# A graph kernel on one core: variance on one row, moved ranges of cells, all equal-key counts in the edge stage

## What is computed

```python
# layer 0: edge convolution, attention mix, norm, mixture of 8 experts
e = relu((x[dst] - x[src]) @ theta.T + phi(x[src]));  out = segment_max(e, dst)   # "runs" of edges
h = layernorm(x_joined);  w = softmax(h @ Wr + br);   y = sum_e w_e * expert_e(h)
# layer 1: three SAGE layers on the same graph
mean = segment_sum(h[src], dst) / max(deg, 1);  h = relu(mean @ Wl + h @ Wr)
```

## Time and profile before

| | before |
|---|---|
| median of 3 runs (lowest, highest) | 2259.45 us (2256.13, 2262.32) |
| the profiled execution: its time / its span | 2258.26 / 2256.5 us |
| busy PE / DVE / POOL / ACT, of the span | 77% / 59% / 50% / 27% |
| granted TensorE clock, mean over the span | 0.85 |
| cells: `DMA_INDIRECT` L715 | 400, 1311 ns each |
| gathers: `DMA_INDIRECT` L281 | 400, 1237 ns each |

### The profile page before, as it was taken

One profiled execution on the slowest core, in us unless ns is written; L12 is line 12 of the kernel. 1 busy time (PEld: TensorE's weight loads), 2 busy tenths in 40 slices (PEclk: granted clock), 3 DMA queues, 4 the chain that ended last, 5 costly groups with the idle time before them and its releaser, 6 DMA issues. The chain is left out here.

```text
span 2256.5 us, 25514 instructions
## 1 busy us (share of the span) xinstructions
PE 1740.6 (77%) x8349; PEld 1011.8 (45%) x8349; DVE 1320.1 (59%) x2672; ACT 598.0 (27%) x940; POOL 1122.8 (50%) x888
## 2 busy tenths in 40 slices
PE   7984645544553658999999628699989999996996
PEld 6962222211222434555555427555565555544543
DVE  6877866776674666777777515445541221125996
ACT  4001101110110135666666312211220010003453
POOL 0868888888885737888888768400000000000344
PEclk9557877777775669999999858799999999997998
DMA  6346788878886202111220200344325433431002
GB/s 173 85 134 195 212 225 230 216 216 219 217 215 163 54 10 61 35 34 34 34 34 9 67 1 2 52 103 109 100 50 130 124 95 92 127 80 38 0 4 82
DMA packets 193283, 229.05 MB, mean 102 GB/s; under 512 B 66688, under 2 KB 174292, under 8 KB 187811
## 3 DMA queue, kind: packets, MB, share of 16 engines
q1 hardware_dynamic: 126001, 172.58, 29.0%
q0 software_dynamic: 67200, 55.46, 11.1%
HBM read 148.81 MB, written 78.24 MB: 101 GB/s over the span
## 5 line engine op out<-in xcount | busy, mean ns | idle before, releaser
L715 POOL DMA_INDIRECT adjacency<-all_cell_val,all_cell_idx x400 | 524.5, 1311 | 173.5 <-issue 121.0
L281 POOL DMA_INDIRECT edge_ring<-b_rows,all_src_idx x400 | 494.8, 1237 | 187.0 <-issue 168.1
L1742 POOL TENSOR_TENSOR ffn_hl<-ffn_hid,ffn_hh 128x448 f16<-128x448 f32 x56 | 70.1, 1254 | 717.3 <-ACT ffn_hid L1759 717.1
L1555 PE MATMUL bank<-sage_adj,sage_zh 125*128 125x448 f16 x1050 | 370.1, 352 | 3.4 <-DVE sage_zl L1609 3.4
L1555 PE MATMUL bank<-sage_adj,sage_zl 125*128 125x448 f16 x1050 | 370.0, 352 | 0.0
L535 DVE SCALAR_TENSOR_TENSOR edge_ring<-edge_ring,w_keep 125x256 f32<-125x256 f32 x399 | 193.0, 484 | 128.6 <-DMA edge_ring<-b_rows,all_src_idx 112.8
L1201 ACT ACTIVATE bank<-bank,w_shift,w_scale 128x448 f32<-128x448 f32 x224 | 147.1, 697 | 76.7 <-PE bank L728 76.7
L1632 DVE TENSOR_TENSOR sage_u<-bank,w_rd 128x448 f32<-128x448 f32 x42 | 26.2, 625 | 236.2 <-PE bank L1560 233.4
L1555 PEld LDWEIGHTS bank<-sage_adj,sage_zh 125*128 125x128 f16 x1050 | 102.6, 98 | 101.9 <-issue 8.0
L1555 PEld LDWEIGHTS bank<-sage_adj,sage_zl 125*128 125x128 f16 x1050 | 102.7, 98 | 99.6 <-issue 5.8
L690 DVE SCALAR_TENSOR_TENSOR edge_junk<-bank,all_key_c,all_later 125x400 f16<-125x400 f32 x232 | 145.7, 628 | 0.0
(11 more groups left out here) (433 smaller groups left out, 3448.3 us busy)
## 6 DMA issues: line engine op xcount, KB each, us to landing
sage_adj<-adjacency SPq DMA_DIRECT2D x105, 490.0 KB
run_max<-edge_ring SPq DMA_DIRECT2D x40, 1120.0 KB
adjacency<-edge_zero SPq DMA_DIRECT2D x25, 714.0 KB
experts_gb<-gate_rows SPq DMA_DIRECT2D x56, 224.0 KB, 3.3
edge_ring<-b_rows,all_src_idx POOLq DMA_INDIRECT x400, 7.1
adjacency<-all_cell_val,all_cell_idx POOLq DMA_INDIRECT x400, 2.6
sage_adj<-adjacency SPq DMA_DIRECT2D x105, 56.9 KB
run_max<-edge_ring SPq DMA_DIRECT2D x40, 130.0 KB
```

The lines of the kernel that those rows point to most:

```text
L281: nc.gpsimd.indirect_dma_start(ring[:, k % RING, :], None, dram.rows[:, :], bass.IndirectOffsetOnAxis(ap=c.src_idx[:, k:k + 1], axis=0)).t ...
L715: nc.gpsimd.indirect_dma_start(dram.adj_flat, bass.IndirectOffsetOnAxis(ap=c.cell_idx[:, k:k + 1], axis=0), c.cell_val[:, k:k + 1], None). ...
L1555: ins = mm(ps[4 * b + h][:, 0:T], z[:, g * JG + j, half(h)], adj[g][:, j, :], start=(g == 0 and j == 0 and z is zh), stop=False)
L1742: nc.gpsimd.tensor_tensor(hl[:, m, :], hid[:, m, :], hh[:, m, :], ALU.subtract).then_inc(low, 1)
```

## The change

1. In the edge stage DVE does all 400 counts, 1.18 for each scan from number 60 on in place of 0.68. When count 320 has been issued, `make_cells` is called for columns 0 to 319 (FIRST = 320), and after the last scan for the other 80.
2. The experts stage has no counts, no `make_cells` and no wait of POOL for them.
3. The ranges of cells: 56 columns in the join (46 before), 254 beside the experts (244), 58 beside norm2 (45), 32 beside mix1 (65).
4. The variance of the join: PE multiplies the squares as weights with one column of `mean_w`, so that a group of 4 blocks gives 125x4 numbers in place of 128x500. ACT's root goes to `sd`, DVE's reciprocal to `rs` (125x4), and PE spreads `rs` with 4 transposes into bank 4, for which DVE's scaling waits (`rs_spread`).

```diff
-JOINED = 46
-LATE = 3 * NT * NEXP
+JOINED = 56
...
-    COUNTS = L - LATE
-    counts_by = lambda k: (k - SCANS) * COUNTS // (L - SCANS)
+    FIRST = 320
+    counts_by = lambda k: (k - SCANS) * L // (L - SCANS)
...
                         count_equal(v, dve, c, ps[3][0:B, 0:L], j, j, junk[:, j % 2, :], counted)
+                        if j == FIRST:
+                            dve.wait_ge(counted, FIRST + 2)
+                            make_cells(v, count_step, c, cell[:], dup[:], slice(0, FIRST))
...
-                make_cells(v, count_step, c, cell[:], dup[:], slice(0, COUNTS))
+                dve.wait_ge(counted, L + 2)
+                make_cells(v, count_step, c, cell[:, FIRST - L:], dup[:, FIRST - L:], slice(FIRST, L))
...
-                        if g >= 1:
-                            act.wait_ge(scaled, g)
-                        nc.scalar.activation(ps[4][:, 0:wide(g)], ps[3][:, 0:wide(g)], ACT.Sqrt, bias=c.eps5[:, 0:1]).then_inc(sd_ready, 1)
+                        if g >= 2:
+                            act.wait_ge(rs_ready, g - 1)
+                        nc.scalar.activation(sd[:, g % 2, 0:size(g)], ps[3][0:B, 0:size(g)], ACT.Sqrt, bias=c.eps5[0:B, 0:1]).then_inc(sd_ready, 1)
...
-                        v.reciprocal(ps[4][:, 0:wide(g)], ps[4][:, 0:wide(g)]).then_inc(rs_ready, 1)
+                        if g >= 2:
+                            dve.wait_ge(rs_spread, g - 1)
+                        v.reciprocal(rs[:, g % 2, 0:size(g)], sd[:, g % 2, 0:size(g)]).then_inc(rs_ready, 1)
...
-                        dve.wait_ge(rs_ready, g + 1)
+                        dve.wait_ge(rs_spread, g + 1)
...
+                    if t >= 3:
+                        g = t - 3
+                        pe.wait_ge(rs_ready, g + 1)
+                        if g >= 1:
+                            pe.wait_ge(scaled, g)
+                        for j in range(size(g)):
+                            ins = nc.tensor.transpose(ps[4][:, B * j:B * (j + 1)], rs[:, g % 2, j:j + 1].to_broadcast([B, P]), c.ident[0:B, 0:B])
+                        ins.then_inc(rs_spread, 1)
...
-                        product(nc, ps[3][:, 0:wide(g)], [c.mean_w[:]] * KH, [sq[:, k, 0:wide(g)] for k in range(KH)]).then_inc(var_done, 1)
+                        for j in range(size(g)):
+                            ins = product(nc, ps[3][0:B, j:j + 1], [sq[:, k, B * j:B * (j + 1)] for k in range(KH)], [c.mean_w[:, 0:1]] * KH)
+                        ins.then_inc(var_done, 1)
...
-                        if steps == K:
-                            for i in range(3 * e, 3 * e + 3):
-                                count_equal(v, dve, c, c.key_c[:], 3 * K * t + i + L - LATE, 3 * K * t + i, junk[:, i % 2, :], counted)
-                    if steps == K:
-                        step.turn(t, 7)
-                        dve.wait_ge(counted, 3 * K * t + 3 * K + 2)
-                        make_cells(v, step, c, cell[:], dup[:], bass.ds(L - LATE + 3 * K * t, 3 * K))
-                        dve.sem_inc(made, 1)
...
-            experts(nc, c, w, dram, made, lambda pool: place_cells(nc, c, dram, pool, JOINED, 290, made))
+            experts(nc, c, w, dram, lambda pool: place_cells(nc, c, dram, pool, JOINED, 310))
...
-                norm(nc, c, 2, lambda pool: place_cells(nc, c, dram, pool, 290, 335), [
+                norm(nc, c, 2, lambda pool: place_cells(nc, c, dram, pool, 310, 368), [
...
-            mix1(nc, c, w, qT, ctx, lambda pool: place_cells(nc, c, dram, pool, 335, L))
+            mix1(nc, c, w, qT, ctx, lambda pool: place_cells(nc, c, dram, pool, 368, L))
```

More of the change, by code:

```diff
@@ L184, in edges @@
             sb = lambda name, shape, dt=F32: late.enter_context(nc.sbuf_tensor(f"cells_{name}", shape, dt))
-            cell, dup = sb("cell", [B, COUNTS]), sb("dup", [B, COUNTS])
+            cell, dup = sb("cell", [B, FIRST]), sb("dup", [B, FIRST])
         free = c.a.rearrange("p k n -> p (k n)")
@@ L672, in _ @@
                     v.tensor_tensor_scan(full[:, h, :], w.reset[:], ps[h][:, 0:B], -BIG, ALU.min, ALU.max).then_inc(ends_scanned, 1)
-                dve.wait_ge(counted, COUNTS + 2)
-                make_cells(v, count_step, c, cell[:], dup[:], slice(0, COUNTS))
+                dve.wait_ge(counted, L + 2)
+                make_cells(v, count_step, c, cell[:, FIRST - L:], dup[:, FIRST - L:], slice(FIRST, L))
 def take(nc, act, c, ps, turned, taken, g, n):
@@ L703, in make_cells, with place_cells @@
     step(v.tensor_tensor(c.cell_val[:, at], c.cnt[:, at], dup, ALU.mult))
-def place_cells(nc, c, dram, pool, first, last, made=None):
-    per = LATE // NT
+def place_cells(nc, c, dram, pool, first, last):
     for k in range(first, last):
-        if made and k >= L - LATE and (k - L + LATE) % per == 0:
-            pool.wait_ge(made, (k - L + LATE) // per + 1)
         if k >= WP * PB and k % WP == 0:
@@ L890, in join_norm_gate @@
         br = s.sb("br", [B, NEXP])
+        sd, rs = s.sb("sd", [B, 2, 4]), s.sb("rs", [B, 2, 4])
         br_in, hot_ready, spread = s.sem("br_in"), s.sem("carry_hot"), s.sem("carry_spread")
@@ L894, in join_norm_gate @@
         mean_done, centred, sq_ready, var_done = s.sem("mean_done"), s.sem("centred"), s.sem("sq_ready"), s.sem("var_done")
-        sd_ready, rs_ready, scaled = s.sem("sd_ready"), s.sem("rs_ready"), s.sem("scaled")
+        sd_ready, rs_ready, rs_spread, scaled = s.sem("sd_ready"), s.sem("rs_ready"), s.sem("rs_spread"), s.sem("scaled")
         high, lowed, logits = s.sem("y_high"), s.sem("y_low"), s.sem("logits")
@@ L1107, in _, with experts @@
                     ins.then_inc(w_turned, 1)
-def experts(nc, c, w, dram, made, beside):
+def experts(nc, c, w, dram, beside):
     with Scope(nc, "experts") as s:
@@ L1115, in experts @@
         gT = s.sb("gT", [NEXP, T])
-        junk = s.sb("junk", [B, 2, L], F16)
-        cell, dup = s.sb("cell", [B, LATE // NT]), s.sb("dup", [B, LATE // NT])
-        counted, own_c = s.sem("counted"), s.sem("cell_steps")
         h1h, h1l = s.sb("h1h", [P, 2, KH, T], F16), s.sb("h1l", [P, 2, KH, T], F16)
@@ L1262, in tile @@
                             ins.then_inc(dm, 1)
-                        if steps == K:
-                            for i in range(3 * e, 3 * e + 3):
-                                count_equal(v, dve, c, c.key_c[:], 3 * K * t + i + L - LATE, 3 * K * t + i, junk[:, i % 2, :], counted)
-                    if steps == K:
-                        step.turn(t, 7)
-                        dve.wait_ge(counted, 3 * K * t + 3 * K + 2)
-                        make_cells(v, step, c, cell[:], dup[:], bass.ds(L - LATE + 3 * K * t, 3 * K))
-                        dve.sem_inc(made, 1)
-                dve.sem_inc(counted, 2)
-                step = Steps(dve, own_c)
                 tile(0)
@@ L1922, in build @@
                                                 pieces(f[0], w.Wo, mats[2])), plan)
-            made = g.sem("cells_made")
-            experts(nc, c, w, dram, made, lambda pool: place_cells(nc, c, dram, pool, JOINED, 290, made))
+            experts(nc, c, w, dram, lambda pool: place_cells(nc, c, dram, pool, JOINED, 310))
         with Scope(nc, "w2") as g:
```

## The result

| | before | changed |
|---|---|---|
| median of 20 runs (lowest, highest) | 2260.73 us (2256.13, 2264.1) | 2266.74 us (2262.07, 2270.86) |
| ratio, 95% interval | 1 | 1.0026 (1.0019 to 1.0032) |
| the profiled execution: its time / its span | 2258.26 / 2256.5 us | 2269.08 / 2267.3 us |
| busy PE / DVE / POOL / ACT, of the span | 77% / 59% / 50% / 27% | 77% / 57% / 50% / 26% |

What follows compares the result with a forecast made beforehand. Bounds differed by stage: POOL in edges, norm2 and mix1, a ring of engines in the join, nearly a tie in experts. Terms 1.4 - 15.5 + 24.4 - 11.1 = -0.8 us gave 2258.7 us, range 2250 to 2270.

Steps and rivals of the forecast that it cites:

- The counts among the gathers: Edge stage: added counts mostly fit in DVE's waits for gathers; +1.4 us, bounds 0 and +20.
- The join: Join: narrow reciprocal and root, transposes beneath DVE's join, less a clock loss; -15.5 us, bounds -8 and -20.5.
- In one or two of five: Join: share of iterations where PE's clock rises late, each losing 2.1 us; taken as +3 us.
- Experts: Experts: POOL's 254 columns plus holds end the stage; +6.9 us, less 1.9 of waiting.
- 30 us of holds: Experts: POOL calls held by 56 subtractions, by laying calls 1.49 us apart; POOL ends 410 us after its start.
- the 1.9 us that it waited beyond a barrier of 2.9 are gone: End of experts: POOL, now last, no longer waits beyond the barrier; -1.9 us.
- norm2: norm2, bounded by POOL alone: 13 more columns at 1.49 us; +19.4 us.
- mix1: mix1: with 32 columns POOL is out of the way, and DVE and a 2.9 us barrier end it; -11.1 us.
- The columns keep their 1.65 us: Rival, experts: POOL ends 420 us after its start, not 410; +9.9 us, 2268.6; chance 0.10.
- Counts hold the gathers: Rival, edge stage: counts hold POOL's gathers as they hold columns; 10 us added, 2268.7; chance 0.05.
- The clock falls behind: Rival, join: PE's clock is late in every iteration; saving 8, not 15.5 us, 2266.2; chance 0.12.
- stays up: Rival, join: PE's clock stays up as idle time shrinks; saving 20.5 us, 2253.7; chance 0.10.

Runs made afterwards that it cites:

- Experiments 5: Changed kernel with the 1.6 MB load of the carry rows issued ten scans earlier; ratio 0.9987 to the kernel before.
- 6: Changed kernel with the same 400 counts done by scan 370, none among the last 30 scans; ratio 0.9986 to the kernel before.
- 10: Changed kernel with one SBUF input, not two, in the operation making the join's low parts; ratio 0.9994 to the kernel before.
- experiment 7: Changed kernel with the experts' subtraction (two SBUF inputs) replaced by a multiplication by 0.0 with one; ratio 0.9958 to the kernel before.
- 8: Changed kernel with columns split 56 join, 246 experts, 36 norm2, 62 mix1; 2228.6 us, ratio 0.9862 to the kernel before.
- experiment 1: Changed kernel with the ranges and wide variance of before, so only the counts moved; ratio 1.0007 to the kernel before.
- experiments 2: Kernel before with only the narrow variance added; ratio 0.9907 to the kernel before.
- 4: Changed kernel with the old ranges (46, 244, 45, 65 columns); ratio 0.9928 to the kernel before.

## Why the prediction was wrong, point by point

**The counts among the gathers: +1.4 forecast, +7.5 in the trace.** This is one of the two steps that failed. The prices and DVE's wait were right (34 us left, 39 forecast). Wrong was "DVE's largest lag grows by about 1.5 us, and its last scan is 0.9 us later". I laid the new scans against the landings of the old trace, as if these were fixed. They are not: the load that starves the gathers is issued behind scan 370, and with DVE later it was issued at 654.38 in place of 648.20. The long wait then ended 8.9 us later (672.52 against 663.61), 20 scans before the end, and each of these scans costs DVE 1.1 us of the 1.5 that POOL gives it: 0.4 us won back by each, 8 in all, for a lag that had just grown by the wait. All eight traces with 400 counts and this tail have a wait of 3.8 to 8.0 us with 21 to 23 scans left and none of over 1 us in the last 20; all three with 232 counts have two or three there. Experiments 5 and 6 show it from two sides, the load moved or the tail bare: waits come back near the end, so DVE had caught up. The size varies by execution: the last scan came 5.0, 5.2 and 5.4 us after the last call in the three kernels with 232 counts, and 5.8 to 9.6 (mean 7.6) in the eight with 400 and an unchanged tail; the stage took 696.2 (694.3 to 698.7) against 700.5 us (696.3 to 703.2) in the mean. So the counts cost about 4 us in this stage, and 7.5 in the trace shown; how much of the difference between the two is chance stays open.

**The join: -15.5 forecast, -14.4.** The size was right, its make-up was not. The other engines gained 21.0 us (130.0 against 151.0 up to the last low part), above my bound of 20.5, and POOL gave 6.6 back with a mechanism that I had seen beside the experts and not looked for here: its ten more columns reach into four operations with two SBUF inputs. The long call is 5.7 of the 6.6. I had POOL end 15 us after 813.5, so at 828.5, or 836 with the later start of the join; it ended at 839.97. The long call (5.55 to 6.89 us) is in all four traces in which POOL was still placing then, and in none of the six others with 56 or 50 columns, where POOL was done. That these operations cause it is argued from that and from where the calls end: 1.06 to 1.07 us after the end of the third operation in three traces (0.26 before the end of the fourth), after the end of the fourth in the one of 6.89, by the same rule as beside the experts. Why the call does not get in between the first and the second stays open; the kernel that was to show the cause (10) missed the place. "In one or two of five" for the slow clock held in the two traces of the changed kernel; of the first five variances one and two ran wholly at half clock there, up to four in the other narrow joins. The variance of the changed kernel at 784.80 us, and the next reciprocals:

```profile
784.80 3.36 PE L764 MATMUL bank<-all_mean_w,join_sq 128*125 128x1 f32 x16
...
788.49 0.18 DVE L1007 RECIPROCAL join_rs<-join_sd 125x4 f32<-125x4 f32 x1 [7.31 <-ACT join_sd L947]
```
```profile
801.91 0.18 DVE L1007 RECIPROCAL join_rs<-join_sd 125x4 f32<-125x4 f32 x1 [5.94 <-ACT join_sd L947]
```

3.36 us is half clock (granted 0.50); at full clock the wide variance took 1.84. The two iterations that took 16.7 us each take 13.4 to 15.1, with the clock down in all or most of them. But the two before them, 18.1 and 17.6 us in the wide form, take 10.8 to 17.1, by whether the clock is up (17.1 where the variance that ends them is at half clock): there is the gain that I had not forecast, and most of the spread of 136 to 145 us among the narrow joins.

**Experts: +5.0 forecast, +12.7.** The second step that failed, by two sizes. "30 us of holds" was 36.8 here, and 29.8 to 32.8 in four other executions with the same 254 columns without counts. POOL took 416.0 us here, 408.8 to 412.0 in those, where I had said 410: the middle was met and I left it no spread. That was partly luck. Laid again by what the traces show (a call that begins within the operation ends 1.06 us after it), calls 1.49 us apart give 22 us of holds against the 56 starts of the trace with counts, which I had used, and 38 against those of the changed kernel; why the other executions have 30 to 33 the laying does not tell. Nor does the phase run freely: 32 of the 49 calls that begin in the subtraction do so 0.04 to 0.13 us after its start, since the fourth call after such a one again falls just behind the next start, 6.81 us later.

And "the 1.9 us that it waited beyond a barrier of 2.9 are gone" was wrong: POOL is idle 4.63 us though it is last, hardly less than its 4.84 before. So this step was wrong in every execution: the experts took 413.4 to 420.6 us in the five traces, 415.9 in the mean, +8.0 for the +5.0 forecast. DVE starts 3.92 us after POOL's last call (1264.80 less 1260.88), but 1.13 to 1.30 after its own last work where it is last (mix1 here, the experts of experiments 7 and 8). So the end of a call of POOL is not yet its arrival at the barrier, and POOL had in effect been last before too: DVE had been idle 2.20 us there, not 1.3. First before, then experiment 7:

```profile
1259.03 0.08 DVE L839 MEMSET all_a<- 128x22 f16 x1 [2.20 <-PEq L83]
```
```profile
1248.42 0.08 DVE L838 MEMSET all_a<- 128x22 f16 x1 [1.30 <-PEq L82]
```

The counts' own holds, 10 us by my laying, were small: in the trace of before 3.2 of the 39.0 us fall on the calls (16) that met a count and not the subtraction. But without counts the other calls fall elsewhere too, and POOL's time fell by 5.7 us in experiment 1 and, for 244 columns, from 403.7 to 391.9 between experiments 2 and 4. That the subtraction holds the calls is shown by where they end, and by experiment 7: 36.8 us became 7.1. The Trainium skill, SBUF — State Buffer, section "Who interferes with whom", says that a VectorE instruction with at most one SBUF input outside the modes with two ports leaves GpSimd alone. The trace agrees for inputs from PSUM: none of 137 calls was held by a count with its keys there. The multiplication of experiment 7, with one SBUF input, held all 27 that began in it; whether it ran in such a mode no run here shows.

**norm2: +19.4 forecast, +19.5.** 13 columns at 1.49 us in a stage that POOL alone holds. Right.

**mix1: -11.1 forecast, -13.4.** Right in mechanism; I took 2.9 us for the barrier after DVE, and DVE is idle only 1.13 us.

**The rivals.** "The columns keep their 1.65 us" nearly came true in the first trace, 1.64 (416.0/254), and less in the others, 1.61 to 1.62. "Counts hold the gathers": POOL's calls are busy 3.1 us more in the edge stage, 1.7 in the mean of the eight traces, not 10, and by scans, not by counts. "The clock falls behind" came true for two iterations, "stays up" for two others. In sum: 6.1 and 7.7 us too little (edges, experts), 1.1 too much gain for the join, 0.1 too little for norm2, and 2.3 and 1.0 us of the other sign (mix1, the rest), which turns the -0.8 of the forecast into +10.9, and the spans differ by 10.9. Of these 10.9 us some 5 to 9 are this pair of executions and not the change, since the medians of the two sets differ by 6.0 and 1.2 to 1.8.

## What to carry to other kernels

Where one stream of work is laid against the waits of another, look at what comes last, not at the sum of the waits: a wait that is made good in the middle of a stage is paid in full when a large load falls 20 steps before its end, and a later consumer may itself issue that load later. Where many calls meet a periodic operation, ask where a held call ends and where the next ones then fall, and give the size a spread. When a stage gets shorter, look again at what the engine beside it will now meet at its end. And a column of work costs what its stage's last engine makes it cost: 30 columns taken out of two stages that POOL ended and put into one where DVE did gave 32 to 38 us.

## What the runs showed of the hardware

An indirect DMA call of POOL that began while certain DVE operations ran ended 1.06 us after the operation, whenever it had begun: all 49 calls within the subtraction of 128x896 (two SBUF inputs, 1.08 us) beside the experts of the changed kernel, and all 27 within a multiplication with one SBUF input (0.62 us) in experiment 7. The 16 calls that were already running when the subtraction began (for 0.18 to 1.03 us) took no longer than usual, nor did any that began within a count with one input in PSUM. One that began 0.14 to 0.16 us after the first of four operations with two SBUF inputs (1.20 us each, copies from PSUM between them) did not end behind the first or the second: it took 5.55 to 5.56 us three times, to 1.07 after the third, and 6.89 once, to 1.07 after the fourth, where 1.19 is usual. The same of one long operation, in mix1 of the kernel before (POOL beside DVE's 3.49 us, ending 1.06 us after it):

```profile
1404.60 3.49 DVE L1382 TENSOR_TENSOR mix_qt<-mix_qt,mix_qm 125x3200 f32<-125x3200 f32 x1
...
1404.82 4.33 POOL L715 DMA_INDIRECT adjacency<-all_cell_val,all_cell_idx  x1 [0.30 <-issue]
```

Behind a load of 1.6 MB issued by SP, DVE waited up to 8.27 us for a gather of POOL's queue. And one kernel, measured in two sets, gave 1.0026 (1.0019 to 1.0032) and 1.0005 (0.9996 to 1.0014) of before: of differences under some 0.3%, only the stages of several traces tell the cause.
